# A two-layer model kernel on one core: second norm in closed form, earlier convolution and a 15-round search ahead of the scans

## The reference

```
# L0_attn (a state-space block); ln_g, ln_b are weights, K = 4, D = 256, N = 16
Xn     = (X - mean) * rsqrt(var + 1e-5) * ln_g + ln_b          # over the 128
X_main = silu(causal_depthwise_conv4(Xn @ W_up1.T) + conv_b)
pp     = X_main @ W_ll.T + b_ll;   delta = softplus(pp[:, :256]);  B, C = the other 32
H_t    = exp(delta*A) * H_(t-1) + U_t;   y_t = C_t . H_t       # a scan over the 256 steps
out    = X + (y * silu(Xn @ W_up2.T)) @ W_down.T + b_down
# L0_ffn: scores = softmax(x @ Wr); each of 8 experts takes its 512 best tokens of 2048,
#         two matmuls with a GELU, weighted by the score and added at the token
# L1_attn: multi-scale retention, 8 heads;  L1_ffn: 16 experts, 2 per token
```

## Time and profile before

| what | us |
|---|---|
| median of 3 runs | 591.31 (586.75, 591.31, 591.4) |
| span of the profiled execution, first to last instruction | 583.0 |
| opening, up to the first scan | 100.6 |
| PE, DVE, POOL, ACT busy | 511.2, 429.5, 370.7, 325.3 |
| mean granted TensorE clock | 0.949 |

### The profile page before, as it was taken

The page is one execution under the profiler, slowest core; times in us unless marked ns, Lnnn a source line. Parts: engine busy times, 40 slices in busy tenths (PEclk is TensorE's granted clock), DMA queues, the critical chain, the costliest instruction groups (busy, mean ns, idle before and its releaser), DMA issues.

```text
span 583.0 us, 14216 instructions
## 1 busy us (share of the span) xinstructions
PE 511.2 (88%) x4760; PEld 367.7 (63%) x4761; DVE 429.5 (74%) x1068; ACT 325.3 (56%) x790; POOL 370.7 (64%) x335
## 2 busy tenths in 40 slices
PE   2779998769999999999799999978789999999980
PEld 1634344546667677767457677535466799999980
DVE  6836556998999999999985244568767766666664
ACT  2466686945798978978423333217655544444420
POOL 2515873957898999999992777622377434555550
PEclk9999998857999999999889999999799899999995
DMA  7899604050303404404503546689111212221207
GB/s 210 153 236 308 174 1 150 2 205 15 147 3 145 157 13 155 148 16 163 195 20 98 191 127 198 210 275 387 47 58 42 70 41 57 59 57 53 56 9 216
DMA packets 58596, 70.96 MB, mean 122 GB/s; under 512 B 9391, under 2 KB 45830, under 8 KB 55600
## 3 DMA queue, kind: packets, MB, share of 16 engines
q1 hardware_dynamic: 53152, 58.49, 31.7%
q0 software_dynamic: 5392, 11.76, 7.8%
HBM read 50.03 MB, written 21.25 MB: 122 GB/s over the span
## 4 chain that ended last, share of the span: by engine, by line
PE 49%; DVE 19%; POOL 18%; issue 6%; ACT 4%; DMA 3%; SPq 1%; DVEq 0%; POOLq 0%; ACTq 0%
POOL arena L2025 14%; PE banks L1597 8%; PE banks L1584 7%; DVE arena L556 6%; PE banks L1360 5%; PE banks L1232 4%; PE banks L1297 4%; POOL xm L2012 3%; PE banks L1146 3%; PE banks L1156 3%; PE banks L1380 2%; PE banks L1437 2%; DVE hbuf L756 1%; PE banks L1325 1%; PE banks L1301 1%
## 5 line engine op out<-in xcount | busy, mean ns | idle before, releaser
L2025 POOL TENSOR_TENSOR arena<-arena,bd 128x512 f32<-128x512 f32 x125 | 158.2, 1288 | 24.7 <-DVE arena L556 24.0
L556 DVE TENSOR_TENSOR_SCAN arena<-banks,arena 128x256 f32<-128x256 f32 x256 | 156.3, 670 | 2.8 <-PE banks L1146 1.8
L1705 ACT ACTIVATE arena<-delta,nega 128x256 f32<-128x256 f32 x256 | 109.5, 495 | 35.9 <-PE banks L1156 27.8
L2115 POOL DMA_INDIRECT pair_rows<-w1b,xnT x48 | 49.9, 1040 | 58.5 <-DVE w1b L845 51.6
L1597 PE MATMUL banks<-arena,hbuf 128*128 x384 | 54.7, 285 | 0.7 <-issue 0.2
L1584 PE MATMUL banks<-xsT,xm 128*128 128x128 f32 x384 | 51.1, 276 | 0.8 <-DVE acc L819 0.8
L1597 PEld LDWEIGHTS banks<-arena,hbuf 128*128 128x128 f32 x384 | 46.5, 191 | 3.7 <-issue 2.0
L1584 PEld LDWEIGHTS banks<-xsT,xm 128*128 128x128 f32 x384 | 46.6, 192 | 1.2 <-DVE acc L819 1.0
L2063 POOL DMA_INDIRECT expert_rows<-gate,zbuf x32 | 34.4, 1075 | 17.8 <-DVE gate L606 8.9
L1146 PE MATMUL banks<-xnT,xnw 44*128 44x172 f32 x384 | 39.4, 341 | 6.2 <-DVE arena L556 5.3
L827 DVE COPY xm<-bd 128x512 f32 x48 | 20.6, 430 | 32.6 <-issue 31.4
(11 more groups left out here) (303 smaller groups left out, 1023.2 us busy)
## 6 DMA issues: line engine op xcount, KB each, us to landing
bd<-c_rows SPq DMA_DIRECT2D x16, 1024.0 KB, 5.8
expert_rows<-blank SPq DMA_DIRECT2D x8, 1024.0 KB, 9.9
xnT<-expert_rows SPq DMA_DIRECT2D x4, 1024.0 KB, 5.0
bd<-in_w SPq DMA_DIRECT2D x4, 1024.0 KB, 13.1
arena<-in_w SPq DMA_DIRECT2D x4, 1024.0 KB, 13.8
slots_in<-blank POOLq DMA_DIRECT2D x1, 3120.0 KB
xnT<-slots_in SPq DMA_DIRECT2D x48, 65.0 KB
xnw<-expert_rows SPq DMA_DIRECT2D x3, 1024.0 KB, 6.4
```

What stands on the lines that cost most here:

```text
L556: m = V.tensor_tensor_scan(ring[:, s, r, :], dw_view(s)[:, 2 * (s % 2) + r, :], ring[:, s, r, :], 0.0, ALU.add, ALU.mult)
L1705: m = nc.scalar.activation(ring[:, s, r, :], delta[:, half(s), bass.ds(b * L, L)], ACT.Exp, scale=negs[:, half(s), n:n + 1])
L2025: nc.gpsimd.tensor_tensor(ring[:, s, :, :], ring[:, s, :, :], c_view(par, s), ALU.mult).then_inc(S["z_pool"], 1)
L2115: nc.gpsimd.indirect_dma_start(out=yd, out_offset=bass.IndirectOffsetOnAxis(ap=xs[:, u, P:P + 1].bitcast(I32), axis=0), in_=ys[:, u % 4, : ...
```

## The change

- **Second norm in closed form.** x1 has mean 0 and variance v/(v+eps), so z = (x - m) / sqrt(v(1+eps) + eps^2). DVE computes v+eps and v(1+eps)+eps^2, ACT takes one root of both, DVE one reciprocal of both, and DVE writes z2 straight from the rows. The statistics of `xn` are gone. `xn` itself is now written by ACT (`first_norm`), after the turned quarters are out.
- **Rows turned once.** Only z2 is turned. ACT copies the turned quarter twice (`z_out`): into `z2p` and, plain, into `xnT`. The logits come from z's rows and are multiplied on DVE by bn[:, :, 1], the ratio of the two roots, before the softmax.
- **Convolution from the first quarter on.** The first two wide matmuls stand before the turns of quarters 1 and 2; the rest of the turns and all logits are put in at g = 2. The count of round 0 moves from g = 1 to g = 7.
- **15 rounds** in a loop of 5 times 3. Ties are counted at g = 52 and 55.
- **Loads.** The four taps (as one transfer) and W_up1 go out on ACT's queue at the very start; `colv` and `cfs` ahead of the search tables. `wconv` signals after each tap. The write of `xn` and POOL's addition wait for ACT's `xn`, and the addition for the first comparison too.

The core of the diff:

```diff
+SEARCH = 15
-        Z2_BANK = (4, 5, 6, 1)
+        Z2_BANK = (4, 5, 6, 4)
@@ norm_stats
+                if nth == 0:
+                    link.more(V.tensor_scalar(bn[:, t, 9], bn[:, t, 7], 1.0 + EPS, EPS * EPS, ALU.mult, ALU.add))
+                link(V.tensor_scalar(bn[:, t, 8], bn[:, t, 7], EPS, None, ALU.add))
+            def normalize_twice(q):
+                t = slice(4 * q, 4 * q + 4)
+                dve.wait_ge(S["norm_root"], q + 1)
+                link(V.reciprocal(bn[:, t, 10:12], bn[:, t, 8:10]))
+                for k in range(4 * q, 4 * q + 4):
+                    link.more(V.tensor_scalar(z2[:, k, :], acc[:, k, :], bn[:, k, 6:7], bn[:, k, 11:12], ALU.subtract, ALU.mult))
+                dve.wait_ge(S["dve_link"], link.n)
+                dve.sem_inc(S["norm_ready"], 1)
+                link.more(V.tensor_tensor(bn[:, t, 1], bn[:, t, 9], bn[:, t, 10], ALU.mult))
+                V.scalar_tensor_tensor(out=bn[:, t, 0], in0=bn[:, t, 6], scalar=-1.0, in1=bn[:, t, 10],
+                                       op0=ALU.mult, op1=ALU.mult).then_inc(S["shift_ready"], 1)
-            for nth, q, part in ((0, 0, 0), (0, 1, 0), (0, 0, 1), ... (1, 3, 1)):
+            for q, part in ((0, 0), (1, 0), (0, 1), (2, 0), (1, 1), (3, 0), (2, 1), (3, 1)):
@@ softmax_less_max
-                link(V.tensor_reduce(sm[:, 0, :], ps, AX.X, ALU.max))
-                link(V.tensor_tensor(s, ps, bc(sm[:, 0, :], E), ALU.subtract))
+                link(V.tensor_tensor(s, ps, bc(bn[:, :, 1], E), ALU.mult))
+                link(V.tensor_reduce(sm[:, 0, :], s, AX.X, ALU.max))
+                link(V.tensor_tensor(s, s, bc(sm[:, 0, :], E), ALU.subtract))
-            with dve.Fori(0, ROUNDS // 4) as j:
+            with dve.Fori(0, SEARCH // 3) as j:
@@ SyncE
+            sp.dma_start(colv[:, :], cols).then_inc(S["ld_c"], 16)
             sp.dma_start(wr0s[:, :], wr0).then_inc(S["ld_r"], 16)
+            sp.dma_start(cfs[:, :], cf[:, P:P + 514]).then_inc(S["ld_c"], 16)
-            for k in range(K):
-                sp.dma_start(convb[:, k, :], conv_t[k, :].partition_broadcast(P)).then_inc(S["ld_w"], 16)
-            sp.dma_start(wup1, w_up1).then_inc(S["ld_w"], 16)
-            sp.wait_ge(S["norm_ready"], 4)
+            sp.wait_ge(S["norm2_ready"], 4)
@@ TensorE
+            def turn_z(q):
+                pe.wait_ge(S["norm_ready"], q + 1)
+                if q > 2:
+                    pe.wait_ge(S["ps_free"], 2)
+                for r in range(4):
+                    m = pe.transpose(bank[Z2_BANK[q]][:, r * P:(r + 1) * P], z2[:, 4 * q + r, :], ident[:, :])
+            def logits0(q):
+                pe.wait_ge(S["ps_free"], 2 * q + 2)
+            def opening(g):
+                if g == 1:
+                    turn_z(1)
+                if g == 2:
+                    turn_z(2)
+                    logits0(0)
+                    turn_z(3)
+                    for q in range(1, 4):
+                        logits0(q)
-            COUNT_AT = (1, 4, 7, 10, 13, 16, 19, 23, 26, 29, 32, 35, 39, 42, 45, 48)
+            COUNT_AT = (7, 10, 13, 16, 19, 22, 25, 28, 31, 34, 37, 40, 43, 46, 49)
@@ widen(j)
+                    if j == 0 and q == 0:
+                        turn_z(0)
+                    if q == 0:
+                        pe.wait_ge(S["ps_free"], 2 * j + 1)
+                            if j == 0 and q == 0:
+                                pe.wait_ge(S["wconv_ready"], k + 1)
+                            rank(14 * j + 4 * q + k)
@@ ScalarE
+            act.dma_start(convb[:, :, :].rearrange("p k e -> p (k e)"), conv_t.rearrange("k e -> (k e)").partition_broadcast(P)
+                          ).then_inc(S["ld_cv"], 16)
+            act.dma_start(wup1, w_up1).then_inc(S["ld_cv"], 16)
+            norm_root(0, 0)
+            norm_root(0, 1)
+            z_out(0)
+            norm_root(0, 2)
+            z_out(1)
+            norm_root(0, 3)
+            nc.scalar.activation(sm[:, 3, 0:1], colv[:, C_EPS:C_EPS + 1], ACT.Exp)
+            z_out(2)
+            z_out(3)
             link.more(nc.scalar.activation(onesb[:, :], ones_f, ACT.Copy))
             link(nc.scalar.activation(ltri[:, :], cfs[:, 257:385], ACT.Copy))
+            for q in range(2):
+                first_norm(q)
             act.wait_ge(S["dve_link"], dve_at["smax0"])
             nc.scalar.activation(sc[:, :, 0:E0], sc[:, :, 0:E0], ACT.Exp).then_inc(S["sm_exp"], 1)
+            for q in range(2, 4):
+                first_norm(q)
@@ GpSimd
-            pool.wait_ge(S["ld_w"], 7 * 16)
+            pool.wait_ge(S["ld_cv"], 2 * 16)
             for k in range(K):
-                m = nc.gpsimd.tensor_tensor(wconv[:, k, :], wup1, convb[:, k, :], ALU.mult)
-            m.then_inc(S["wconv_ready"], 1)
+                nc.gpsimd.tensor_tensor(wconv[:, k, :], wup1, convb[:, k, :], ALU.mult).then_inc(S["wconv_ready"], 1)
-            pool.wait_ge(S["norm_ready"], 4)
+            pool.wait_ge(S["norm2_ready"], 4)
+            pool.wait_ge(S["cnt_in"], 1)
             nc.gpsimd.tensor_tensor(acc[:, :, :], acc[:, :, :], xn[:, :, :], ALU.add).then_inc(S["sum_ready"], 1)
```

More of the change, by code:

```diff
@@ L375, in _ @@
             z2 = hbuf[:, 0, :, :].rearrange("p c (q d) -> p (c q) d", d=P)
[L376 to L384, removed]
-                else:
-                    if nth == 0:
-                        dve.wait_ge(S[f"rows_at{q}"], 16)
-                    norm_stats(source, nth, q)
+            for q, part in ((0, 0), (1, 0), (0, 1), (2, 0), (1, 1), (3, 0), (2, 1), (3, 1)):
+                if part:
+                    normalize_twice(q)
+                else:
+                    dve.wait_ge(S[f"rows_at{q}"], 16)
+                    norm_stats(acc, 0, q)
+            dve.wait_ge(S["dve_link"], link.n)
             dve.sem_inc(S["dve_done"], 2)
@@ L417, in _ @@
             dve.wait_ge(S["ld_s"], 32)
-            with dve.Fori(0, ROUNDS // 4) as j:
-                link.loop(j, 24)
-                for r in range(4):
-                    i = j * 4 + r
+            with dve.Fori(0, SEARCH // 3) as j:
+                link.loop(j, 18)
+                for r in range(3):
+                    i = j * 3 + r
                     link(V.tensor_tensor(cand[:, :, :], thr[:, None, :].broadcast_to([P, 3, E0]),
@@ L434, in _ @@
                     link(V.tensor_tensor(thr[:, :], thr[:, :], gain[:, :], ALU.bitwise_or))
-            link.end(ROUNDS // 4)
+            link.end(SEARCH // 3)
             thf = thr[:, :].bitcast(F32)
@@ L1031, in transpose_norm @@
                 m.then_inc(S["ps_ready"], 1)
-            for q in range(5):
-                if q < 4:
-                    pe.wait_ge(S["norm_ready"], q + 1)
-                    transpose_norm(q)
-                if q:
-                    pe.wait_ge(S["ps_free"], q)
-                    if q == 1:
-                        pe.wait_ge(S["ld_r"], 16)
-                    for t in range(4 * q - 4, 4 * q):
-                        m = pe.matmul(bank[7][:, t * E0:(t + 1) * E0], xnT[:, t * P:(t + 1) * P], wr0s[:, :], start=True, stop=True)
-            m.then_inc(S["pe_done"], 1)
-            z2 = hbuf[:, 0, :, :].rearrange("p c (q d) -> p (c q) d", d=P)
-            for q in range(4):
-                pe.wait_ge(S["norm2_ready"], q + 1)
+            def turn_z(q):
+                z2 = hbuf[:, 0, :, :].rearrange("p c (q d) -> p (c q) d", d=P)
+                pe.wait_ge(S["norm_ready"], q + 1)
+                if q > 2:
+                    pe.wait_ge(S["ps_free"], 2)
                 for r in range(4):
@@ L1050, in _ @@
                 m.then_inc(S["ps_ready"], 1)
-            pe.wait_ge(S["ld_w"], 7 * 16)
-            pe.wait_ge(S["wconv_ready"], 1)
-            pe.wait_ge(S["ps_free"], 8)
+            def logits0(q):
+                pe.wait_ge(S["ps_free"], 2 * q + 2)
+                if q == 0:
+                    pe.wait_ge(S["ld_r"], 16)
+                for t in range(4 * q, 4 * q + 4):
+                    m = pe.matmul(bank[7][:, t * E0:(t + 1) * E0], xnT[:, t * P:(t + 1) * P], wr0s[:, :], start=True, stop=True)
+                if q == 3:
+                    m.then_inc(S["pe_done"], 1)
+            def opening(g):
[7 more added lines that the diff above has]
+                        logits0(q)
             def count(i):
@@ L1618, in norm_root @@
                 act.wait_ge(S["dve_link"], dve_at[nth, q])
-                nc.scalar.activation(bn[:, 4 * q:4 * q + 4, 9], bn[:, 4 * q:4 * q + 4, 8], ACT.Sqrt).then_inc(S["norm_root"], 1)
+                t = slice(4 * q, 4 * q + 4)
+                if nth == 0:
+                    nc.scalar.activation(bn[:, t, 8:10], bn[:, t, 8:10], ACT.Sqrt).then_inc(S["norm_root"], 1)
+                else:
+                    nc.scalar.activation(bn[:, t, 9], bn[:, t, 8], ACT.Sqrt).then_inc(S["norm_root"], 1)
             def turned_out(q, first):
```

76 lines of the change are left out of this document (35 added, 41 removed).

## The result

The change makes the kernel faster: 572.48 us median of 4 runs (572.0 to 577.06) against 589.03 of 4 (585.48 to 591.4), ratio 0.9744 with a 95% interval of 0.9694 to 0.9794. A second set gave 574.63 against 585.89 (17 runs of before), ratio 0.9787 (0.9732 to 0.9842).

What follows compares the result with a forecast made beforehand. Three bounds in turn: the norm chain to 35 us, PE's stream with the search to about 87, ACT's chain to 89.34. A lead of 8.6 off the 591.3 us median gave 582.7 us, range 577 to 588.5.

Steps and rivals of the forecast that it cites:

- the term of 8.3 us in the sum: End of the sum: run times of before lay a median 8.3 us above the profiled span, carried to the new kernel.
- The lead itself: First scan 8.6 us earlier than before, at 92.0, and that lead kept to the end of the span.
- Rows late by 1.0, bounds 0 and 2.2: Opening loads: rows land 1.0 us later because 640 KB of taps and W_up1 are asked for at the same moment.
- POOL beside DVE, 1.0: Norms: POOL's four products for `wconv` slow DVE's tiles beside them by 1.0 us, bounds 0 and 2.8.
- The cold start paid as before, turns 1.12, logits 1.87: PE's opening: 1.12 us per quarter's turns, 1.87 for a quarter's logits, then two wide matmuls at half speed, 3.4 us.
- ACT sets `steps(0)`, just: Start of `steps(0)`: ACT's silus end at 36.5 us, PE gets there at 36.3, so PE waits for ACT.
- Loop turns and the extra count, -1.2: PE's stream, g = 14 to 41: three loop turns at 0.5 us less 0.46 cost 1.0, one more count 0.2.
- Ties one matmul later, -0.9: End of the search: ties one wide matmul later delay the places and so the first scan by 0.9 us.
- 15 rounds free; fills hidden; scans untouched and the lead kept to the end: Dropped round costs nothing at either end; SP's fills, to about 75 us, stay hidden; scans and all behind unchanged.
- the prediction's own list: Signs to check in the new profile; a first scan before 89 or after 96 us would show the prediction wrong.
- A: Rival, more gain (0.25): loads and `wconv` leave DVE undisturbed, +2.0, loop turns hidden behind ACT, +1.2: 579.5 us.
- B: Rival, little gain (0.15): ten matmuls from g = 4 to 13 run at half clock, lead of 1.6 us: 589.7 us.

Runs made afterwards that it cites:

- with the clock held: 21 matmuls of 128x256 whose result nobody reads, added to the kernel before and to the one after: 585.63 us and 572.17 us.
- The run with all turns first: The changed kernel with all turns and logits ahead of the first wide matmul, without the early convolution: median of five runs 580.83 us.
- the repeat: The changed kernel run and profiled once more with nothing altered: 574.63 us.
- the sixteen-round kernel: The changed kernel with the 16th search round back, loop of 4 times 4, ties at g = 54 and 55: 584.36 us.

## Why the prediction was wrong

**The step that failed most: the term of 8.3 us in the sum.** "The three runs lay 3.7 to 8.4 above the span, the median 8.3" took one execution's span and other runs' times for one thing, and carried the 8.3 over to the new kernel. A run's time is its own span plus 1.8 us. The profile of before showed an execution of 584.8 us, near the fast end of a kernel that scatters from 582.8 to 595 over its 44 later runs. In the new kernel the median lies 2.3 above the profiled span (572.48 and 570.2). The miss of 10.2 us is therefore 6.0 from this term (8.3 against 2.3) and 4.2 from the span (574.4 forecast, 570.2 measured). Set on the profiled run's own time, the forecast would have been 584.8 - 8.6 = 576.2, for a profiled run of 572.04.

The 591.31 itself was no outlier: the median of all 48 runs of before is 589.9, that of the ten of after 573.3. These two medians are 16.5 us apart (16.6 and 11.3 in the two sets by themselves), the two profiled spans 12.8. No run of before above 590 was profiled, so where it loses its time is not known.

**The lead itself was mis-sized: 8.6 forecast, 11.6 at the first scan (12.0 with the clock held), 12.8 at the end of the span.** The lead was forecast at 10.7 at g = 14, 9.5 at ACT's release and 8.6 at the first scan; it was 11.6, 10.8 and 11.6. So of the 3.0 us missing at the first scan 0.9 come from the opening, 0.4 from the loop and 1.7 from the ties. The remaining 1.2 lie behind it, where the prediction had put nothing. By its steps:
- *Rows late by 1.0, bounds 0 and 2.2.* Measured 3.4 in the profile of after (7.20 against 3.76) and 2.4 in the least of the five with two queues, outside the bounds in all. Bytes over rate was no upper bound for a transfer that shares the engines. The rule of the Trainium skill ("DMA: Bandwidth & Descriptors", "Queues, rings and completion order") gave the right sign, and the 0.9 us worked out from it in equal bytes was well under half of what came. It speaks of packets and not of bytes; that the taps' 4 KB pieces weigh more than the rows' 512 bytes would fit, but no run here varied the piece.
- *POOL beside DVE, 1.0.* Measured 1.2 (2.35 against 1.12). Right.
- *The cold start paid as before, turns 1.12, logits 1.87.* Wrong, and the largest term the other way: turns and first logits at half the time, since the two early wide matmuls had raised the clock. The run with all turns first puts the early start at 3.9 to 4.8 us; the prediction had counted two matmuls only. From the last quarter of z to the end of the logits it took 5.0 us instead of 7.9, and z had been 2.3 late, so the logits ended at 26.9 for 27.5: two errors that cancel, which is luck.
- *ACT sets `steps(0)`, just.* In the profile of after it did not; the silus that it waits for ended at 35.5 and PE came at 35.65 without a wait. In the repeat it did, PE waiting 0.97 us. The two lay within 1 us of each other, which is what "just" said.
- *Loop turns and the extra count, -1.2.* Measured -0.8 (a lead of 11.6 at g = 14 and 10.8 at 78.55). ACT's chain of 12.1 stayed, as forecast (12.0).
- *Ties one matmul later, -0.9.* Measured +0.8. In before the two matmuls around the ties ran at half speed after PE's wait for ACT (0.56); in after the same wait of 1.97 was followed by 1.99 us for both, at full speed. With the clock held in both kernels, PE's release to the first scan took 10.06 us in before (89.90 to 99.96) and 10.44 in after (77.52 to 87.96). So the later place does cost, but 0.4 and not 0.9, and the clock of before hid it. With three matmuls' earlier places the gain was 0.5, since DVE's work behind the ties then ran beside POOL's.
- *15 rounds free; fills hidden; scans untouched and the lead kept to the end.* The first held in the kernel before (0.5 us) and not in the changed one, where the round put back cost 2.7 at the first scan. The second held. The third did not hold for single runs: from the first scan to C's third spread the same code took from 44.4 to 52.5 us by its clock.

By the prediction's own list, a first scan before 89 would show it wrong; it came at 88.98, and the rows at 7.2 and the last quarter of z at 21.9 were outside their marks too. Of the rivals, A's time (579.5) was nearest. Its first reason, that the loads and `wconv` leave DVE alone, was false, and its second, that the loop's turns are hidden behind ACT, was borne out in part only. B named the clock, and in the opening five wide matmuls did start at the low level, but they cost no more than the cold start in the forecast. The place where the clock costs most, the first sequence of the scans, was in no rival.

**What stays open.** The medians differ by 13.5 us with the clock held, where the traces show 12.2 at the third spread and 10.5 at the end. In the expert part the distance of the profiles of before and after moves between 10.5 and 13.2 us by itself, and no run separated that. Why the wait of 1.97 us in after left the clock up, and the same wait in the sixteen-round kernel did not (3.66 us for the two matmuls), was not found.

## What to carry to other kernels

Before a forecast is set on a median, ask which run the profile shows, and put the sum on that run's own time. A load moved to a second queue to come earlier competes with the load that starts the chain: here 640 KB cost the rows 2.4 to 3.4 us, and issuing them behind the rows gave 2.1 us back at the first scan (2.5 with the clock held). Here wide matmuls that started early were worth more than their own time to the narrow ones behind them, and a stage in which TensorE waits for others can charge the next one for it.

## What the runs showed of the hardware

- A wait of TensorE of 2 us was followed by the low clock in one profile and not in another: two wide matmuls in 1.99 us after one wait of 1.97, in 3.66 after another.
- Logits of 8 columns, with TensorE busy all the time (6.80 of 6.80 us from 22.7 to 29.5, the last 2.6 of them wide matmuls), ran while the clock fell to 1.2 GHz. In the repeat of the same kernel they ended at full speed and it fell about 1 us later, under 128x512 matmuls (0.50 from 25.9 to 29.0). With one 128x128 matmul after each tile it fell in neither place.
- The first matmuls of a kernel ran at half speed (2.07 us for one of 128x512, later 0.86 from start to start) while the PEclk column read 1.00.
- The rows' first 256 KB landed at 3.54 to 3.93 with one queue at work (nine profiles), and at 6.16 to 7.20 with two (five profiles), though before and after moved the same 180 GB/s over the first 100 us.
- A 128x128 bf16 product on DVE took 0.23 us alone and 1.21 beside GpSimd's products.
